# Decoder layer: the decayed scores of the attention go through three single-pass matmuls over high and low parts of q and k

## What is computed

```python
x = x + attn(layernorm(x))
x = x + xattn(layernorm(x), ctx)
x = x + moe(layernorm(x))

# attn: 16 heads of 128
q, k, v = h @ Wq, h @ Wk, h @ Wv
beta, gate = sigmoid(h @ Wb + bb), silu(h @ Wg)
q = layernorm_per_head(silu(causal_conv4(q)))
k = layernorm_per_head(silu(causal_conv4(k)))
S = (1 - beta_t) * S + beta_t * outer(v_t, k_t)
o_t = S @ q_t
out = (o * gate) @ Wo
```

## Time and profile before

| | us |
|---|---|
| median of 3 runs | 578.58 (578.08 to 578.64) |
| the profiled execution | 578.73 |
| its span, first to last instruction | 576.9 |
| what lies around the span | 1.8 |
| PE busy | 554.7 (96%) |
| DVE busy | 432.5 (75%) |
| ACT busy | 398.1 (69%) |
| POOL busy | 292.7 (51%) |
| mean granted TensorE clock | 0.997 |

### The profile page before, as it was taken

The page is one execution under the profiler, slowest core; times in us unless marked ns, Lnnn a source line. Parts: engine busy times, 40 slices in busy tenths (PEclk is TensorE's granted clock), DMA queues, the critical chain, the costliest instruction groups (busy, mean ns, idle before and its releaser), DMA issues.

```text
span 576.9 us, 9944 instructions
## 1 busy us (share of the span) xinstructions
PE 554.7 (96%) x3392; PEld 485.0 (84%) x3392; DVE 432.5 (75%) x1046; ACT 398.1 (69%) x782; POOL 292.7 (51%) x194
## 2 busy tenths in 40 slices
PE   4898999999999999999999999989899999999997
PEld 1597889989989999899899898878678888888887
DVE  8769989998998899889989998978956543323333
ACT  3979988979779789798797887786653334333431
POOL 2335756746666457366565673420021565556552
PEclk9999999999999999999999999999999999999999
DMA  6132032032030130230211202210020433233321
GB/s 201 31 120 84 0 120 84 1 119 83 3 120 25 59 120 2 82 107 15 84 51 70 83 1 102 82 30 2 1 56 5 164 129 98 95 129 127 94 81 73
DMA packets 18001, 42.31 MB, mean 73 GB/s; under 512 B 4736, under 2 KB 6528, under 8 KB 17952
## 3 DMA queue, kind: packets, MB, share of 16 engines
q1 hardware_dynamic: 17952, 41.69, 21.6%
HBM read 40.47 MB, written 1.21 MB: 72 GB/s over the span
## 4 chain that ended last, share of the span: by engine, by line
PE 85%; DVE 7%; ACT 4%; issue 1%; DMA 1%; SPq 1%; DVEq 0%; ACTq 0%
PE bank L1346 21%; PE bank L1348 20%; PE bank L1347 20%; PE bank L1342 14%; PE bank L1486 5%; PE bank L1474 4%; ACT tok L671 2%; DMA w_raw<-in_w 1%; DVE stats L1051 1%; DVE xT_lo L986 1%; DVE stats L971 1%; DVE x L1187 1%; ACT values L585 1%; DVE x L1336 0%; DVE raw L1070 0%
## 5 line engine op out<-in xcount | busy, mean ns | idle before, releaser
L1346 PE MATMUL bank<-xT_lo,w_hi 128*128 128x512 f32 x320 | 133.7, 418 | 1.9 <-DVE conv L1070 1.2
L1348 PE MATMUL bank<-xT_hi,w_hi 128*128 128x512 f32 x320 | 125.9, 394 | 0.0
L1347 PE MATMUL bank<-xT_hi,w_lo 128*128 128x512 f32 x320 | 125.3, 392 | 0.0
L464 POOL TENSOR_TENSOR gated_lo<-gated,gated_hi 128x512 fp32r<-128x512 f32 x30 | 38.8, 1293 | 116.5 <-ACT gated_hi L691 112.8
L671 ACT ACTIVATE tok<-bank,nmr,rstd 128x128 f32<-128x128 f32 x256 | 91.2, 503 | 2.0 <-DVE nmr L966 2.0
L1346 PEld LDWEIGHTS bank<-xT_lo,w_hi 128*128 128x128 f32 x320 | 60.5, 189 | 16.3 <-DVE conv L1070 3.2
L459 POOL TENSOR_TENSOR raw<-tap,raw 128x506 f32<-128x506 f32 x32 | 62.0, 1936 | 20.3 <-DVE raw L1070 16.3
L459 POOL TENSOR_TENSOR conv<-tap,conv 128x506 f32<-128x506 f32 x32 | 62.0, 1936 | 20.1 <-DVE conv L1070 20.1
L1348 PEld LDWEIGHTS bank<-xT_hi,w_hi 128*128 128x128 f32 x320 | 60.2, 188 | 13.6
L1347 PEld LDWEIGHTS bank<-xT_hi,w_lo 128*128 128x128 f32 x320 | 60.7, 190 | 9.1
L1051 DVE BATCH_NORM_STATS2 stats<-bank 128x6 f32<-128x128 f32 x256 | 56.4, 284 | 14.8 <-PE bank L1474 14.8
(11 more groups left out here) (184 smaller groups left out, 1398.4 us busy)
## 6 DMA issues: line engine op xcount, KB each, us to landing
obet<-obet_rows SPq DMA_DIRECT2D x16, 768.0 KB, 4.3
w_raw<-in_w SPq DMA_DIRECT2D x22, 384.0 KB, 4.8
tap<-route_rows SPq DMA_DIRECT2D x16, 512.0 KB, 4.0
w_raw<-in_w SPq DMA_DIRECT2D x12, 256.0 KB, 3.0
wv_raw<-in_wv SPq DMA_DIRECT2D x8, 256.0 KB, 4.8
wo_raw<-in_wo SPq DMA_DIRECT2D x8, 256.0 KB, 4.9
w_raw<-in_w SPq DMA_DIRECT2D x12, 128.0 KB, 2.1
x<-in_x SPq DMA_DIRECT2D x2, 512.0 KB, 4.7
```

Of the source, the lines that this page charges most:

```text
L464: nc.gpsimd.tensor_tensor(gated_lo[:, cc], gated[:, c * N:(c + 1) * N], gated_hi[:, cc].bitcast(F32), ALU.subtract).then_inc(gated_lo_read ...
L1346: nc.tensor.matmul(o, l_hi, r_lo, start=start, stop=False, skip_group_check=loose)
L1347: nc.tensor.matmul(o, l_lo, r_hi, start=False, stop=False, skip_group_check=loose)
L1348: return nc.tensor.matmul(o, l_hi, r_hi, start=False, stop=stop, skip_group_check=loose)
```

## The change

`scores` no longer multiplies `qk` as float32. ACT rounds q and k of the head to float32r (`high_q`, `high_k`, one activation for each chunk of 512 columns), POOL subtracts to get the low parts (`low_q`, `low_k`), and PE multiplies them with `mm3`: three matmuls with 256 moving columns and three with 128, for each sequence. The parts lie in two slots of `gated_hi` and `gated_lo`: q in that of the head itself, k in the next one. On PE the second chunk of the first projection of head k+2 moves from behind the third `scores` to ahead of the first, and the last `to_tokens` from behind the fourth `scores` to ahead of it. DVE's and SP's order stay as they are.

```diff
--- before.py
+++ after.py
@@ -236,6 +236,15 @@
             return (wv_hi[:, 64:64 + 3 * D], wv_lo[:, 64:64 + 3 * D]) if n == 3 else (
                 wo_hi[:, 0:3 * D], wo_lo[:, 0:3 * D])
 
+        def split_q(hi, k):
+
+
+            return (gated_hi if hi else gated_lo)[:, k % G * T:(k % G + 1) * T]
+
+        def split_k(hi, k):
+            o = (k + 1) % G * T
+            return (gated_hi if hi else gated_lo)[:, o:o + T]
+
         bank = [ctx.enter_context(nc.psum_tensor(f"bank{i}", [P, N], F32)) for i in range(8)]
         a_ring, t_ring, c_ring = bank[0:2], bank[2:6], bank[6:8]
         e_ring, y_acc = bank[0:4], bank[4:8]
@@ -259,6 +268,8 @@
         ld_route = [sem(f"ld_route{i}") for i in range(2)]
         a_full, a_copied, gate_drained = sem("a_full"), sem("a_copied"), sem("gate_drained")
         t_full, t_drained = sem("t_full"), sem("t_drained")
+        q_hi_ready, k_hi_ready = sem("q_hi_ready"), sem("k_hi_ready")
+        q_lo_ready, k_lo_ready = sem("q_lo_ready"), sem("k_lo_ready")
         c_full, c_drained = sem("c_full"), sem("c_drained")
         w_hi_ready, w_lo_ready = sem("w_hi_ready"), sem("w_lo_ready")
         wv_hi_ready, wv_lo_ready = sem("wv_hi_ready"), sem("wv_lo_ready")
@@ -475,6 +486,18 @@
             split_low(0, 0)
             low_values(0, 0)
             split_low(0, 1)
+
+            def low_q(g, k, u):
+                pool.wait_ge(q_hi_ready, units(g, k, NCH, u + 1))
+                nc.gpsimd.tensor_tensor(split_q(False, k)[:, u * N:(u + 1) * N], qk[:, u * N:(u + 1) * N],
+                                        split_q(True, k)[:, u * N:(u + 1) * N].bitcast(F32),
+                                        ALU.subtract).then_inc(q_lo_ready, 1)
+
+            def low_k(g, k, u):
+                pool.wait_ge(k_hi_ready, units(g, k, NCH, u + 1))
+                nc.gpsimd.tensor_tensor(split_k(False, k)[:, u * N:(u + 1) * N], qk[:, T + u * N:T + (u + 1) * N],
+                                        split_k(True, k)[:, u * N:(u + 1) * N].bitcast(F32),
+                                        ALU.subtract).then_inc(k_lo_ready, 1)
             last_tap(0, 0, range(2 * NCH))
 
             def low_shared(g, k):
@@ -499,6 +522,10 @@
                 low_shared(g, k)
                 if has(g, k + 1):
                     last_tap(*head(g, k + 1), (3,))
+                low_q(g, k, 0)
+                low_k(g, k, 0)
+                low_k(g, k, 1)
+                low_q(g, k, 1)
                 if has(g, k - 1):
                     gated_low(*head(g, k - 1), 1)
                 if has(g, k + 2):
@@ -682,6 +709,16 @@
                         act.wait_ge(c_full, c_scores(g, k - 1) + B)
                     nc.scalar.activation(qk[:, u * N:(u + 1) * N], t_ring[u][:, :], ACT.Identity,
                                          scale=prm[:, o:o + 1], bias=prm[:, o + 1:o + 2]).then_inc(t_drained, 1)
+
+            def high_q(g, k, u):
+                act.wait_ge(t_drained, units(g, k, 8, 4 + u + 1))
+                nc.scalar.activation(split_q(True, k)[:, u * N:(u + 1) * N], qk[:, u * N:(u + 1) * N],
+                                     ACT.Copy).then_inc(q_hi_ready, 1)
+
+            def high_k(g, k, u):
+                act.wait_ge(t_drained, units(g, k, 8, 6 + u + 1))
+                nc.scalar.activation(split_k(True, k)[:, u * N:(u + 1) * N], qk[:, T + u * N:T + (u + 1) * N],
+                                     ACT.Copy).then_inc(k_hi_ready, 1)
 
             def gated_high(g, k, c):
 
@@ -761,11 +798,15 @@
                 if has(g, k + 1):
                     gates(*head(g, k + 1), (0,))
                 affine(g, k, (1,))
+                high_q(g, k, 0)
                 if has(g, k + 1):
                     silu(*head(g, k + 1), (1,))
                     gates(*head(g, k + 1), (1,))
                 affine(g, k, (2,))
                 affine(g, k, (3,))
+                high_k(g, k, 0)
+                high_k(g, k, 1)
+                high_q(g, k, 1)
                 if has(g, k + 1):
                     silu(*head(g, k + 1), (2,))
                     silu(*head(g, k + 1), (3,))
@@ -795,7 +836,12 @@
             g, k = NG - 1, 3
             shared_high(g, k)
             normalise(g, k, range(2 * NCH))
-            affine(g, k, range(2 * NCH))
+            affine(g, k, (0, 1))
+            high_q(g, k, 0)
+            affine(g, k, (2, 3))
+            high_k(g, k, 0)
+            high_k(g, k, 1)
+            high_q(g, k, 1)
             gated_high(g, k - 1, 1)
             context_exp(range(G))
 
@@ -1491,12 +1537,15 @@
 
                 for b in some:
 
-                    pe.wait_ge(t_drained, units(g, k, 8, 7 + b // BPC))
+                    pe.wait_ge(k_lo_ready, units(g, k, NCH, 1 + b // BPC))
+                    pe.wait_ge(q_lo_ready, units(g, k, NCH, 1 + b // BPC))
                     pe.wait_ge(c_drained, c_scores(g, k) + (b - 1))
-                    q0, k0 = b * L, T + b * L
-                    mm(c_ring[b % 2][:, 0:L], qk[:, k0:k0 + P], qk[:, q0:q0 + L], True, True)
-                    mm(c_ring[b % 2][:, L:DW], qk[:, k0 + P:k0 + L], qk[:, q0 + P:q0 + L],
-                       True, True).then_inc(c_full, 1)
+                    o = b * L
+                    k_, q_ = (split_k(True, k), split_k(False, k)), (split_q(True, k), split_q(False, k))
+                    mm3(c_ring[b % 2][:, 0:L], *(a[:, o:o + P] for a in k_), *(a[:, o:o + L] for a in q_),
+                        True, True)
+                    mm3(c_ring[b % 2][:, L:DW], *(a[:, o + P:o + L] for a in k_), *(a[:, o + P:o + L] for a in q_),
+                        True, True).then_inc(c_full, 1)
 
             def outputs(g, k, some):
 
@@ -1601,16 +1650,16 @@
                     project_in(*head(g, k + 2), 0, (0,))
                 if has(g, k + 1):
                     to_tokens(*head(g, k + 1), (1,))
+                if has(g, k + 2):
+                    project_in(*head(g, k + 2), 0, (1,))
                 scores(g, k, (0,))
                 scores(g, k, (1,))
                 if has(g, k + 1):
                     to_tokens(*head(g, k + 1), (2,))
                 scores(g, k, (2,))
-                if has(g, k + 2):
-                    project_in(*head(g, k + 2), 0, (1,))
+                if has(g, k + 1):
+                    to_tokens(*head(g, k + 1), (3,))
                 scores(g, k, (3,))
-                if has(g, k + 1):
-                    to_tokens(*head(g, k + 1), (3,))
                 outputs(g, k, (0,))
                 if has(g, k + 2):
                     project_in(*head(g, k + 2), 1, (0,))
```

2 lines of the change are left out of this document (1 added, 1 removed).

## The result

The changed kernel takes 620.1 us (median of four runs, 619.1 to 620.2) where the kernel before, on the same chip, takes 578.6: a ratio of 1.0716, 95% interval 1.0702 to 1.0731, so 7.2% slower. The forecast was 616.0 us, 6.5% slower, in a range of 604 to 624. The profiled execution has a span of 617.4 us, 40.5 more than before.

The account below looks back on a forecast made before the run. Bound: PE, busy 96%, plus a second loop over all engines with under 0.1 us to spare behind `decayed(2)`. Delays of 7 + 24 + 2.7 + 3.6 = 37.3 us on 578.73 gave 616.0 us; range 604 to 624.

Parts of the forecast that it names:

- The matmuls: Scores on PE: six float32r matmuls take 0.684 us a sequence in place of 0.655, +1.9 us over 64 sequences.
- The way from `affine` over POOL: q and k pass ACT, then POOL, before the third scores; `decayed(2)` late by 2.0 us in 12 steps, 24 us.
- The ends: The last two heads, with less or nothing left to overlap: scores late by 2.7 and 3.6 us.
- Head 14: Its third scores come at 375.2 in place of 372.47, +2.7 us.
- Head 15: Last head, nothing left to overlap: its third scores come at 392.35 in place of 388.64, +3.6 us.
- The moved projection chunk: On PE ahead of the first scores: its 1.4 to 1.5 us hide the wait for POOL's first low part of k.
- ACT's three further roundings: 1.6 us of ACT's work a step, beside the late scores; ACT has idle time later, so nothing added.
- The price of 0.218 a matmul: Rival: float32r matmuls of 128 columns cost as much as float32; +5 us, 621 us; 9%.
- PE as sole bound: Rival: PE stays the only bound and all of the delay is hidden; +1.9 us, 580.5 us; 5%.
- the gain: Rival: PE stays the bound and a matmul of 128 columns costs 0.065 us; -6.8 us, 571.8 us; 2%.
- the half absorbed: Rival: idle time of DVE and ACT makes good half of the delay; +19 us, 597 us; 10%.
- POOL and DVE blocking each other: Rival: more POOL operations meet DVE's scan or factors, up to 1.3 us a step; 637 us; 4%.

Follow-up runs that it names:

- order_back: Changed kernel with PE's old order: the projection chunk and the last `to_tokens` back where they were before; 623.6 us, ratio 1.0781.
- f32_no_wait: Changed kernel with float32 scores that wait for `affine` alone; parts still made, PE's new order kept; 602.0 us, ratio 1.0425.
- parts_made_only: Kernel before with the parts of q and k made beside float32 scores that don't wait for them, PE's old order; 587.8 us, ratio 1.0178.
- reordered: Changed kernel, same work, with ACT's, PE's and DVE's instructions behind the parts in another order; 609.3 us, ratio 1.0557.

## Why the prediction was right, and where its reasons were wrong

- **The matmuls, +0.03 us a sequence, +1.9 us on PE and not added.** Right: 0.11 for 128 columns, and +1.9 us when they alone are changed.
- **The way from `affine` over POOL, `decayed(2)` late by 2.0.** Right, at 2.07, with its parts: POOL starts 0.71 behind `high_k(0)`'s start (forecast 0.77), the subtractions stand 1.25 to 1.26 apart, `low_q(1)` ends at 4.50 (4.59), the third scores start at 4.61 (4.70). PE's two waits are 0.48 and 1.01 as idle time and 0.73 and 1.16 between the starts (0.7 and 1.1), and nowhere else in the step. The period is 24.94 (24.9).
- **The ends.** Mis-sized: "Head 14: ... +2.7" and "Head 15: ... +3.6". With the interval between the last two `tok`s at +3.8 and the rest at +4.4, they are 1.1 and 0.8 more. There PE waits 2.6 us for POOL, twice, and the window 395 to 420 has a granted clock of 0.93 and the next one 0.86, where before there was one fall (0.93 in 400 to 423). That was named as an uncertainty and not put into the sum. With the middle, 2.07 a step in place of 2.0 (+0.9), the first two steps (+0.3) and the way to the first `tok` (+0.2) that makes, rounding aside, the 3.2 us by which the span exceeds the 614.2 of the forecast.

```profile
395.00:420.00 25.00, 21.27 (x141) 19.09 (x140) 20.22 (x47) 17.17 (x39) 13.66 (x10) 0.93 0.14 49
420.00:445.00 25.00, 20.73 (x114) 17.95 (x113) 14.35 (x41) 15.60 (x39) 6.24 (x5) 0.86 0.06 17
```

- **"The moved projection chunk ... hidden. Without that chunk it would be a wait of 1.5."** True of the changed kernel (order_back has the wait, 1.20 us in the middle), but taken for more than it says: the chunk is hidden only because the scores are late anyway. By itself it makes the same loop longer by 1.36 us a step, and f32_no_wait shows that the wait for POOL adds only 0.69 to that. The prediction followed one way, the longest one, and gave no price to the second longest. That this left the number right is no merit of the step: in a kernel with a shorter way over POOL the same reasoning would have missed by up to 1.36 us a step.
- **"ACT's three further roundings lie beside this."** Right in the changed kernel, where the longer way covers them; with that way gone they cost 0.26 us a step, as a later `silu` for the transposes (parts_made_only).
- **The rivals.** The price of 0.218 a matmul, PE as sole bound, the gain and the half absorbed are all out by the rows above. POOL and DVE blocking each other did not happen in the changed kernel beyond what was there before (DVE's scan is 3.86 us as in the earlier trace rows). But the small chance hung on the times of one order: a small change of it (reordered) brought the block up at 0.62 us a step.

## What to carry to other kernels

A page on which one engine is busy for 96% can hide a second loop over all engines with the same period and no slack; follow the timelines round one full step, and price whatever is put into that loop at its latency, even where every engine has room. Ways in such a loop do not add up but compete: undo them one at a time and two at a time before one of them is given the blame, or credit for hiding another. A step that is moved ahead "to fill a wait" should be timed alone in the kernel without the wait as well.
